# Two-layer graph network: nine upper products move into the first pass over the adjacency, and GpSimd folds part of the row sums

## The chip, the cores and the metric

The kernel runs on one core of a Trainium2 chip. The metric is the device time of one execution in microseconds. Three runs before the change gave a median of 897.39 (895.74 to 899.43).

## The reference

```python
A = adj + I                                # adj: 4096 x 4096, f32
d = rsqrt(sum(A, axis=1))
x1 = layernorm(x + elu(((A * d[:, None] * d[None, :]) @ x) @ w))
x2 = layernorm(x1 + relu((adj @ x1) @ W.T + b))     # x: 4096 x 256
```

## The kernel before

The 4096 nodes are cut into 8 groups of 512 (32-row blocks are dealt out so that two groups share one panel of 1024). A **chunk** is the part of adj with one row group and one panel of 1024 columns, 2.1 MB, in one of the tiles raw0 to raw2; SyncE and ScalarE each issue two of its four transfers (`load_chunk`, L248). A chunk holds two **units** (row group, column group), 512 by 512 each. There are 64 units in each of the two layers.

A unit goes through three engines. VectorE turns it in 32 by 32 blocks (`turn`, L530, one STREAM_TRANSPOSE). ScalarE copies it to the rounded a_hi (`hi`, L378), and VectorE writes the rest, a_lo (`lo`, L549), two halves each. TensorE makes 24 products of 128x512 into one accumulator (`product`, L802): v_hi with a_hi, v_hi with a_lo, v_lo with a_hi. v is the right factor, in a high and a low part: y = d * (x @ w) in the first layer, x1 in the second. Each of turned, a_hi and a_lo has two buffers, so VectorE runs at most two units ahead of TensorE.

The chunks come in three passes, each a list built at L63 to L94.
- Pass A, chunks 0 to 31, reads all of adj once for the degrees. VectorE sums DVE_BLOCKS blocks of a chunk (`deg_part`, L560) and ScalarE the rest of the 16 (L388). At the end of a row group VectorE adds the parts (`deg_sum`), TensorE folds them over the partitions (`fold_degrees`, L733), VectorE adds 1 (`deg_row`), GpSimd makes d (L336), ScalarE scales x @ w by it and rounds it to v_hi (`make_y`, L398), and VectorE makes v_lo (`v_low`, L582). As row group r gives v of group r, pass A can take the units below the diagonal: those with a column group before the row group, 28 in all, and one diagonal unit, (0, 0). Their accumulators are kept in the tile partial (`keep_partial`, L417). x @ w of a group is made on TensorE in `turn_x` and `project_x`.
- Pass B, chunks 32 to 63, reads all of adj again: the other 35 units of layer 1 complete a row group of x1 each, and behind them come the 28 units of layer 2 below the diagonal.
- Pass C, 20 chunks, does the 36 units of layer 2 on and above the diagonal.

When a row group is complete, VectorE aggregates (L588), TensorE projects it (L764), ScalarE makes the elu, the moments and the normalised rows, GpSimd adds x (L346) and makes the small factors, each at a fixed number of units behind (AGG_AT and the others, L132).

Every engine runs its own list in a written order; semaphores hold an engine until its input is there. SyncE and ScalarE issue the loads of a chunk when the chunk before it in the same buffer has been turned and summed (`raw_free`, L253). SyncE's queue also carries the loads of x, each behind a fixed chunk (L297).

## Time and profile before

| | |
|---|---|
| median of 3 runs | 897.39 us (895.74 to 899.43) |
| the profiled execution | 896.96 us |
| its span, first to last instruction | 894.9 us |
| TensorE (PE) busy | 790.3 us, 88% |
| VectorE (DVE) | 738.4 us, 83% |
| ScalarE (ACT) | 528.5 us, 59% |
| GpSimd (POOL) | 102.5 us, 11% |
| HBM read | 185.2 MB, 212 GB/s over the span |

Busy time is the time in which an engine executes. A matmul is pipelined, so a busy TensorE need not be at its peak. A row of a timeline gives start and duration in us, engine, line (L556 is line 556), the tiles written and read, and in brackets the idle time before it with what ended it. "x2" is two instructions shown together.

### The profile page before, as it was taken

The page shows a single profiled execution, that of the slowest core. Times are in us where ns is not written, and L with a number is a line of the kernel's source. Part 1 is how long each engine was busy: PE and PEld are TensorE (multiplying, and loading weights), DVE is VectorE, ACT ScalarE, POOL GpSimd, SP SyncE. Part 2 cuts the span into 40 slices and gives each one's busy share as a digit, 9 for nine tenths or more (in the row PEclk, how much of TensorE's full clock was granted, in tenths as well). Part 3 has the DMA queues.
Part 4 walks back from the last instruction along what each step waited for, and adds up shares of the span by engine and source line. Part 5 has one row for each costly group of instructions (what it writes and reads, how often), then busy time and mean ns, then how long its engine had stood idle before and what let it go on. Part 6 is the DMA issues. An engine that isn't in the chain of part 4 may idle for free. (4 is left out here: it accounts for less than half of the span.)

```text
span 894.9 us, 10620 instructions
## 1 busy us (share of the span) xinstructions
PE 790.3 (88%) x3532; PEld 650.9 (73%) x3532; DVE 738.4 (83%) x557; ACT 528.5 (59%) x1180; POOL 102.5 (11%) x109
## 2 busy tenths in 40 slices
PE   0166477698999999999999999999999999999996
PEld 0045365577888788888888888888887878888884
DVE  0749478889998889898989889898979889888863
ACT  1447377578877544756667575756744665455361
POOL 0000000000000000211112021110210412022020
PEclk9987698899999999999999999999999999999998
DMA  9999999988975997878888787888895897997800
GB/s 273 305 294 287 304 210 301 276 208 251 247 214 162 237 210 217 194 180 191 225 190 214 191 223 182 192 224 192 200 242 170 193 229 187 222 214 178 222 24 23
DMA packets 192037, 190.09 MB, mean 212 GB/s; under 512 B 7024, under 2 KB 191984, under 8 KB 191984
## 3 DMA queue, kind: packets, MB, share of 16 engines
q1 hardware_dynamic: 98928, 97.40, 42.8%
q10 hardware_dynamic: 93056, 92.03, 41.6%
q8 instruction: 28, 0.46, 0.2%
q14 instruction: 25, 0.20, 0.1%
HBM read 185.20 MB, written 4.19 MB: 212 GB/s over the span
## 5 line engine op out<-in xcount | busy, mean ns | idle before, releaser
L820 PE MATMUL acc<-a_hi,v_hi 128*128 128x512 f32 x1024 | 408.3, 399 | 17.5 <-DVE a_lo L556 13.3
L385 ACT ACTIVATE a_hi<-turned 128x1024 fp32r<-128x1024 f32 x256 | 264.5, 1057 | 260.9 <-PE acc L822 130.1
L821 PE MATMUL acc<-a_lo,v_hi 128*128 128x512 f32 x1024 | 402.9, 393 | 0.0
L822 PE MATMUL acc<-a_hi,v_lo 128*128 128x512 f32 x1024 | 402.7, 393 | 0.0
L539 DVE STREAM_TRANSPOSE turned<-raw 128x2048 f32<-128x2048 f32 x128 | 294.1, 2305 | 46.1 <-DMA raw<-in_adj_dram 39.0
L556 DVE TENSOR_TENSOR a_lo<-turned,a_hi 128x1024 fp32r<-128x1024 f32 x256 | 301.9, 1217 | 33.2 <-ACT a_hi L385 16.7
L820 PEld LDWEIGHTS acc<-a_hi,v_hi 128*128 128x128 f32 x1024 | 195.1, 191 | 61.9 <-issue 17.3
L822 PEld LDWEIGHTS acc<-a_hi,v_lo 128*128 128x128 f32 x1024 | 194.8, 190 | 41.3
L821 PEld LDWEIGHTS acc<-a_lo,v_hi 128*128 128x128 f32 x1024 | 195.2, 191 | 39.8
L395 ACT ACTIVATE acc<-raw 128x256 f32<-128x256 f32 x236 | 87.0, 368 | 27.7 <-issue 22.3
L563 DVE TENSOR_REDUCE deg_parts<-raw 128x10 f32<-128x2560 f32 (+4 forms) x32 | 77.9, 2442 | 9.5 <-DMA raw<-in_adj_dram 9.5
L346 POOL TENSOR_TENSOR raw<-raw,x_row 128x1024 f32<-128x1024 f32 x8 | 22.1, 2761 | 223.3 <-ACT raw L441 223.3
L739 PE MATMUL acc<-deg_sums,fold 128*32 128x4 f32 x64 | 2.1, 194 | 48.5 <-DVE deg_sums L572 48.5
L395 ACT ACTIVATION_READ_ACCUMULATOR acc<-raw 128x1 f32 x236 | 44.3, 188 | 0.0
L336 POOL TENSOR_TENSOR dinv<-deg,minus_half 128x4 f32<-128x4 f32 x8 | 11.0, 1375 | 283.4 <-DVE deg L580 283.4
L585 DVE TENSOR_TENSOR v_lo<-normed,v_hi 128x1024 fp32r<-128x1024 f32 x16 | 19.6, 1224 | 25.1 <-ACT v_hi L474 17.5
L739 PEld LDWEIGHTS acc<-deg_sums,fold 128*32 128x32 f32 x64 | 1.4, 124 | 51.0 <-DVE deg_sums L572 50.6
L458 ACT ACTIVATE raw<-raw,minus_mean 128x256 f32<-128x256 f32 x60 | 29.8, 499 | 12.2 <-issue 6.4
L470 ACT ACTIVATE normed<-raw,shift,rstd 128x256 f32<-128x256 f32 x60 | 31.2, 591 | 6.3 <-POOL shift L368 6.3
L359 POOL TENSOR_SCALAR minus_mean<-sums 128x4 f32<-128x4 f32 x15 | 9.6, 643 | 219.4 <-ACT raw L452 219.4
L760 PE MATMUL proj<-w_sb,x_row 128*128 128x256 f32 x128 | 30.5, 393 | 1.1 <-ACT x_row L414 1.1
L760 PEld LDWEIGHTS proj<-w_sb,x_row 128*128 128x128 f32 x128 | 25.1, 198 | 5.1 <-ACT x_row L414 1.4
(56 smaller groups left out, 353.0 us busy)
## 6 DMA issues: line engine op xcount, KB each, us to landing
raw<-in_adj_dram SPq DMA_DIRECT2D x168, 512.0 KB, 8.8
raw<-in_adj_dram ACTq DMA_DIRECT2D x168, 512.0 KB, 9.8
x_row<-in_x_dram SPq DMA_DIRECT2D x64, 128.0 KB, 6.7
out_dram<-normed ACTq DMA_DIRECT2D x28, 128.0 KB, 3.1
w_sb<-in_L_gnn_w_dram SPq DMA_DIRECT2D x1, 256.0 KB, 15.7
normed<-in_L_gnn_W_dram SPq DMA_DIRECT2D x1, 256.0 KB, 14.1
out_dram<-normed SPq DMA_DIRECT2D x4, 64.0 KB, 1.8
out_dram<-normed ACTq DMA_DIRECT2D x4, 64.0 KB, 1.9
```

Of the source, the lines that this page charges most:

```text
L346: nc.gpsimd.tensor_tensor(res, res, x_row[:], ALU.add).then_inc(s_resx, 1)
L385: nc.scalar.activation(a_hi[u % 2][:, part, :], turned[u % 2][:, part, :], ACT.Copy).then_inc(s_hi, 1)
L395: nc.scalar.activation(junk[:, i % JUNK, :], raw[buffer_of[n]][:, k, :], ACT.Copy, accum_out=deg_parts[:, row % 2, panel, k:k + 1]).then_i ...
L458: nc.scalar.activation(neg[:, t, :], res[:, t, :], ACT.Square, bias=minus_mean[:, t:t + 1], accum_out=squares[:, t:t + 1]).then_inc(s_sq, 1)
L470: nc.scalar.activation(normed[:, t, :], res[:, t, :], ACT.Identity, scale=rstd[:, t:t + 1], bias=shift[:, t:t + 1]).then_inc(s_norm, 1)
L539: ins = nc.vector.transpose(dst, src)
L556: nc.vector.tensor_tensor(a_lo[u % 2][:, part, :], turned[u % 2][:, part, :], a_hi[u % 2][:, part, :].bitcast(F32), ALU.subtract).then_inc ...
L563: nc.vector.tensor_reduce(deg_parts[:, row % 2, panel, mine], raw[buffer_of[n]][:, mine, :], AX_X, ALU.add).then_inc(s_degd, 1)
L760: ins = pe.matmul(proj[:, t, :], flat[:, GN * h + P * t:GN * h + P * (t + 1)], w_sb[:, h, :], start=(h == 0), stop=(h == CH - 1))
L820: pe.matmul(dst, v_hi[:, k, ch], a_hi[u % 2][:, t, :], start=begin, stop=False)
L821: pe.matmul(dst, v_hi[:, k, ch], a_lo[u % 2][:, t, :], start=False, stop=False)
L822: ins = pe.matmul(dst, v_lo[:, k, ch], a_hi[u % 2][:, t, :], start=False, stop=end)
```

## The change

Pass A takes ten of the units on and above the diagonal, those whose row and column group are both below 4 (one of them, (0, 0), was there before); so it has 38 units and pass B 54 of two layers in 28 chunks. FIRST_UNITS is the table of what is done at which chunk. A unit above the diagonal is done at a later chunk than its own, when v of its column group exists. Its chunk is kept until then: chunks (0, 1), (1, 1), (0, 0) and (2, 1) lie in three further places, in the upper parts of v_hi, v_lo and partial that pass A does not use before, and others stay in a rotating buffer for up to two chunks more. Six accumulators are added onto a partial that is there already (`add_partial`, VectorE).

In groups 0 to 3, `make_y` and the low half of v (`y_low`) come at the end of the own row group, since the last unit needs them. v_hi is written from PSUM in one step, and v_lo by four operations that scale x @ w again. From group 2 on GpSimd adds halves of four of the 16 blocks of each chunk in three steps (256 columns to 32, `fold_part`), and VectorE reduces what is left (`deg_of_pool`). VectorE has 10, 10, 8, 6, 5, 6, 6, 5 blocks per row group in place of 10, 10, 10, 9, 9, 8, 7, 6, and ScalarE 6, 6, 4, 6, 7, 6, 6, 7 in place of 6, 6, 6, 7, 7, 8, 9, 10. ScalarE issues its share of a load by a list, `loads_at`.

```diff
+    FAST = 4
     chunks = []
     units = []
     accs = []
-    def add_chunk(name, row, panel, columns):
-        chunks.append((name, row, panel, []))
+    visits = []
+    def add_unit(name, row, col, n, visit):
+        layer = 0 if name == "A" or (name == "B" and col >= row) else 1
+        if not accs or accs[-1][:3] != (name, row, layer):
+            accs.append((name, row, layer, len(units), None))
+        accs[-1] = accs[-1][:4] + (len(units),)
+        visits[visit].append(len(units))
+        units.append((name, row, col, n, len(accs) - 1))
+    def add_chunk(name, row, panel, columns=()):
+        chunks.append((name, row, panel))
+        visits.append([])
         for col in columns:
-            layer = 0 if name == "A" or (name == "B" and col >= row) else 1
-            if not accs or accs[-1][:3] != (name, row, layer):
-                accs.append((name, row, layer, len(units), None))
-            accs[-1] = accs[-1][:4] + (len(units),)
-            chunks[-1][3].append(len(units))
-            units.append((name, row, col, len(chunks) - 1, len(accs) - 1))
-    DIAGONALS = 1
-    ORDER_A = [[1, 2, 3, 0], [1, 2, 3, 0], [2, 0, 3, 1], [2, 0, 3, 1], [2, 0, 3, 1], [0, 3, 1, 2], [0, 3, 1, 2],
+            add_unit(name, row, col, len(chunks) - 1, len(chunks) - 1)
+    ORDER_A = [[1, 2, 3, 0], [1, 2, 3, 0], [0, 2, 3, 1], [0, 2, 3, 1], [2, 0, 3, 1], [0, 3, 1, 2], [0, 3, 1, 2],
                [0, 1, 2, 3]]
+    FIRST_UNITS = {3: [(0, 0)], 7: [(1, 0)], 8: [(1, 1)], 9: [(0, 1), (2, 0)], 10: [(2, 1)], 12: [(2, 2)],
+                   13: [(0, 2), (1, 2)], 14: [(3, 0), (3, 1)], 15: [(3, 2)], 16: [(3, 3), (0, 3)],
+                   17: [(1, 3), (2, 3)], 18: [(4, 0), (4, 1)], 19: [(4, 2), (4, 3)]}
     for row in range(GROUPS):
         for panel in ORDER_A[row]:
-            add_chunk("A", row, panel, [col for col in (2 * panel, 2 * panel + 1)
-                                        if col < row or col == row < DIAGONALS])
-    for row in range(GROUPS):
-        own = row // 2
-        for panel in ([*range(own + 1, PANELS), own, *range(own)] if row else range(PANELS)):
-            both = [col for col in (2 * panel, 2 * panel + 1) if not col == row < DIAGONALS]
-            add_chunk("B", row, panel, both[::-1] if panel == own and row % 2 else both)
+            add_chunk("A", row, panel)
+    chunk_of = {(row, panel): n for n, (_, row, panel) in enumerate(chunks)}
+    for n, (_, row, panel) in enumerate(list(chunks)):
+        here = FIRST_UNITS.get(n, []) if row <= FAST else [(row, c) for c in (2 * panel, 2 * panel + 1) if c < row]
+        for r, col in here:
+            add_unit("A", r, col, chunk_of[r, col // 2], n)
+    LATE = range(FAST // 2, PANELS)
+    for row, panels in ((0, LATE), (1, LATE), (2, LATE), (1, (0,)), (3, LATE), (2, (0,)), (4, (3, 2)), (3, (0, 1)),
+                        (4, (0, 1)), (5, (3, 2, 0, 1)), (6, (3, 0, 1, 2)), (7, (3, 0, 1, 2))):
+        for panel in panels:
+            both = [c for c in (2 * panel, 2 * panel + 1) if row >= FAST or panel in LATE or c < row]
+            add_chunk("B", row, panel, both[::-1] if panel == row // 2 and row % 2 else both)
...
+    adds = [a for a, s in enumerate(accs) if s[0] == "A" and any(k[:2] == s[:2] for k in accs[:a])]
+    partials = [a for a in range(len(accs)) if a not in rows_done and a not in adds]
...
+    HOMES = {chunk_of[0, 1]: 3, chunk_of[1, 1]: 4, chunk_of[0, 0]: 5, chunk_of[2, 1]: 5}
     buffer_of, before, filled = [], [], []
-    for n, c in enumerate(chunks):
-        buffer_of.append(n % 3 if n <= THIRD + 2 else (n - THIRD - 1) % 2)
-        held = [k for k in range(n) if buffer_of[k] == buffer_of[n]]
+    for n in range(len(chunks)):
+        if n in HOMES:
+            home = HOMES[n]
+        else:
+            held = [max([k for k in range(n) if buffer_of[k] == i], default=-1) for i in range(3)]
+            free = [(done_at[k] if k >= 0 else -1, i) for i, k in enumerate(held)]
+            home = min(free[:3 if n <= FIRST_B else 2])[1]
...
+    AHEAD = 3
+    loads_at = [[] for _ in chunks]
+    for n in range(AHEAD, len(chunks)):
+        loads_at[max(n - AHEAD, -1 if before[n] is None else done_at[before[n]])].append(n)
+    DVE_BLOCKS = [10, 10, 8, 6, 5, 6, 6, 5]
+    POOL_BLOCKS, POOL_FROM = 4, 2 * PANELS
+    ACT_BLOCKS = [RB - d - (POOL_BLOCKS if row >= 2 else 0) for row, d in enumerate(DVE_BLOCKS)]
...
+        late = FAST * GT * C
+        raw.append(nc.alloc_sbuf_tensor_at("held0", [P, RB, STRIPE], F32, offset=v_at + 4 * late))
+        raw.append(nc.alloc_sbuf_tensor_at("held1", [P, RB, STRIPE], F32, offset=v_at + 4 * (N // P * C + late)))
+        raw.append(partial[:, FAST:, :, :].rearrange("p g h n -> p (g h n)").rearrange("p (b m) -> p b m", b=RB))
...
+                if n >= POOL_FROM:
+                    eng.wait_ge(s_halved, n - POOL_FROM + 1)
...
+                    n = PANELS * m + (1 if m < FAST else 2)
...
+            def fold_part(n):
+                i = n - POOL_FROM
+                raw_loaded(pool, n)
+                mine = raw[buffer_of[n]][:, RB - POOL_BLOCKS:, :]
+                if i:
+                    pool.wait_ge(s_quartered, i)
+                nc.gpsimd.tensor_tensor(halved[:], mine[:, :, :STRIPE // 2], mine[:, :, STRIPE // 2:], ALU.add).then_inc(s_halved, 1)
+                pool.wait_ge(s_halved, i + 1)
+                if i:
+                    pool.wait_ge(s_folded, i)
+                nc.gpsimd.tensor_tensor(quartered[:], halved[:, :, :STRIPE // 4], halved[:, :, STRIPE // 4:], ALU.add).then_inc(s_quartered, 1)
+                pool.wait_ge(s_quartered, i + 1)
+                if i >= 2:
+                    pool.wait_ge(s_degp, i - 1)
+                nc.gpsimd.tensor_tensor(folded[:, i % 2, :, :], quartered[:, :, :STRIPE // 8], quartered[:, :, STRIPE // 8:],
+                                        ALU.add).then_inc(s_folded, 1)
...
+            for n in range(FIRST_B):
+                row, at = divmod(n, PANELS)
+                if n >= POOL_FROM:
+                    fold_part(n)
+                if row < FAST and at == PANELS - 1:
+                    make_dinv(row)
+                if row > FAST and at == 0:
+                    make_dinv(row - 1)
...
                 act.wait_ge(s_xw, row + 1)
-                if row:
-                    act.wait_ge(s_v, row)
+                if row >= FAST:
+                    act.wait_ge(s_turn, max(units_through[n] for n in HOMES))
                 for t in range(GT):
-                    ins = nc.scalar.activation(normed[:, t, :], proj[:, t, :], ACT.Copy,
+                    ins = nc.scalar.activation(v_hi[:, tiles(row).start + 2 * t, :], proj[:, t, :], ACT.Copy,
                                                scale=dinv[:, GT * row + t:GT * row + t + 1])
-                ins.then_inc(s_yf, 1)
-                act.wait_ge(s_yf, row + 1)
-                nc.scalar.activation(v_hi[:, tiles(row), :], normed[:], ACT.Copy).then_inc(s_vhi, 1)
+                ins.then_inc(s_vhi, 1)
...
+            for n in range(AHEAD):
+                load_chunk(act, n, (2, 3))
+            for n in range(FIRST_B):
+                row, at = divmod(n, PANELS)
+                summed_first = row < FAST and at == PANELS - 1
+                if summed_first:
+                    raw_loaded(act, n)
+                    deg_part(n)
+                if n == PANELS - 1:
+                    make_y(row)
+                for u in visits[n]:
+                    hi_and_later(u)
+                    if u == visits[n][0] and row > FAST and at == Y_AT:
+                        make_y(row - 1)
+                if not visits[n] and row > FAST and at == Y_AT:
+                    make_y(row - 1)
+                if not summed_first:
+                    raw_loaded(act, n)
+                    deg_part(n)
+                load_others(n)
+                if summed_first and n > PANELS:
+                    make_y(row)
+                if at == (2 if row < FAST else 3):
+                    keep_xt(row)
+            for n in range(FIRST_B, len(chunks)):
+                for u in visits[n]:
+                    if u == visits[n][-1]:
+                        load_others(n)
...
+            def y_low(row):
+                dve.wait_ge(s_vhi, row + 1)
+                for t in range(GT):
+                    k = tiles(row).start + 2 * t
+                    ins = nc.vector.scalar_tensor_tensor(out=v_lo[:, k, :], in0=proj[:, t, :],
+                                                         scalar=dinv[:, GT * row + t:GT * row + t + 1],
+                                                         in1=v_hi[:, k, :].bitcast(F32), op0=ALU.mult, op1=ALU.subtract)
+                ins.then_inc(s_v, 1)
+            def add_partial(a):
+                row = accs[a][1]
+                dve.wait_ge(s_used, halves_of(accs[a][4], 1))
+                dve.wait_ge(s_part, partial_of[next(k for k in partials if accs[k][:2] == accs[a][:2])] + 1)
+                if add_of[a]:
+                    dve.wait_ge(s_padd, add_of[a])
+                nc.vector.tensor_tensor(partial[:, row, :, :], acc[bank_of[a]][:], partial[:, row, :, :],
+                                        ALU.add).then_inc(s_padd, 1)
 
             def v_low(i, row):
...
+            def turn_and_low(u):
+                turn(u)
+                if u:
+                    low_and_later(u - 1)
             dve.wait_ge(s_const, 1)
 
-            for n, (name, row, panel, mine) in enumerate(chunks):
-                done, at = divmod(n, PANELS)
-                last = done - 1
-                if 0 <= last < GROUPS and at == (1 if last < DIAGONALS else 3):
-                    v_low(last, last)
+            for n in range(FIRST_B):
+                row, at = divmod(n, PANELS)
+                if n > POOL_FROM and at:
+                    deg_of_pool(n - 1)
+                if 0 < row <= FAST and at == 0:
+                    y_low(row - 1)
+                if row > FAST and at == 3:
+                    y_low(row - 1)
+                if row < FAST and at == PANELS - 1:
+                    raw_loaded(dve, n)
+                    deg_part(n)
+                    deg_sum(row)
+                    if row < 2:
+                        deg_row(row)
+                    for u in visits[n]:
+                        turn_and_low(u)
+                        low_and_later(u)
+                    if row >= 2:
+                        deg_row(row)
+                else:
+                    for u in visits[n]:
+                        if units[u][3] == n:
+                            raw_loaded(dve, n)
+                        turn_and_low(u)
+                    raw_loaded(dve, n)
+                    deg_part(n)
+                    if n == 1:
+                        keep_wt()
+                    if row > FAST and at == 0:
+                        deg_row(row - 1)
+                    if visits[n]:
...
+            for n in range(FIRST_B):
+                row, at = divmod(n, PANELS)
+                if row < FAST and at == 2:
+                    turn_x(row)
+                if row < FAST and at == 3:
+                    project_x(row)
+                    fold_degrees(row)
+                for u in visits[n]:
+                    if row >= FAST and u == last_in_a[row]:
                         fold_degrees(row)
                     product(u)
-                    for a in ended(u, PROJECT_AT, rows_done):
-                        project(a)
-                if name == "A" and n % PANELS == (1 if row < DIAGONALS else 2):
+                if row >= FAST and at == 2:
```

In the order of instructions on VectorE, row group 3 of pass A (chunks 12 to 15) reads as follows before. L580 is deg of group 2, L585 the low half of v for group 2.

```order
L563 TENSOR_REDUCE deg_parts<-raw 128x9
L580 TENSOR_SCALAR deg<-acc 128x4
L539 STREAM_TRANSPOSE turned<-raw 128x2048 x2
L556 TENSOR_TENSOR a_lo<-turned,a_hi 128x1024 x2
L563 TENSOR_REDUCE deg_parts<-raw 128x9
L556 TENSOR_TENSOR a_lo<-turned,a_hi 128x1024 x2
L563 TENSOR_REDUCE deg_parts<-raw 128x9
L585 TENSOR_TENSOR v_lo<-normed,v_hi 128x4x256
L539 STREAM_TRANSPOSE turned<-raw 128x2048
L563 TENSOR_REDUCE deg_parts<-raw 128x9
```

The end of group 2 and the first two chunks of the same group 3 after the change. L672 is deg of group 2, L679 its low half, L652 the reduction of what GpSimd folded, held_49 and held_50 the chunks kept in v_hi and v_lo.

```order
L664 TENSOR_REDUCE deg_sums<-deg_parts 128x16
L672 TENSOR_SCALAR deg<-acc 128x4
L679 SCALAR_TENSOR_TENSOR v_lo<-proj,dinv,v_hi 128x256 x4
L621 STREAM_TRANSPOSE turned<-partial 128x2048
L628 TENSOR_TENSOR turned<-turned,ident 128x4x32 x4
L645 TENSOR_REDUCE deg_parts<-raw 128x6
L638 TENSOR_TENSOR a_lo<-turned,a_hi 128x1024 x2
L652 TENSOR_REDUCE deg_parts<-folded 128x4
L621 STREAM_TRANSPOSE turned<-held_49 128x2048
L621 STREAM_TRANSPOSE turned<-held_50 128x2048
L638 TENSOR_TENSOR a_lo<-turned,a_hi 128x1024 x2
```

The low half has moved from behind three chunks' reductions to the place right behind deg, ahead of the first transpose of group 3.

On ScalarE, the same place before: x_row is kept, the first chunk of group 3 summed, two units of a_hi, a partial, a sum, a load, and then `make_y` (L405, L409) of group 2.

```order
L414 ACTIVATE x_row<-proj 128x1024
L395 ACTIVATE acc,deg_parts<-raw 128x256 x7
L251 DMA raw<-in_adj_dram 32x16x256 x2
L385 ACTIVATE a_hi<-turned 128x1024 x4
L423 ACTIVATE partial<-acc 128x1024
L395 ACTIVATE acc,deg_parts<-raw 128x256 x7
L251 DMA raw<-in_adj_dram 32x16x256 x2
L405 ACTIVATE normed<-proj,dinv 128x256 x4
L409 ACTIVATE v_hi<-normed 128x4x256
```

And after: chunk 11 is summed from partial, and `make_y` (L472) of group 2 follows it.

```order
L479 ACTIVATE x_row<-proj 128x1024
L462 ACTIVATE acc,deg_parts<-partial 128x256 x4
L287 DMA raw<-in_adj_dram 32x16x256 x2
L472 ACTIVATE v_hi<-proj,dinv 128x256 x4
L452 ACTIVATE a_hi<-turned 128x1024 x2
```

`make_y` stands ahead of all of group 3's units, and its second step is gone.

## Rows read from the trace of the kernel before

**Rows 1.** The page, TensorE's busy tenths in 40 equal slices of the span.
```profile
PE   0166477698999999999999999999999999999996
```

**Rows 2.** Busy us by engine (x instructions), TensorE's clock, DMA share, GB/s, three stretches.
```profile
50.00:175.00 125.00, 77.71 (x333) 62.46 (x332) 88.34 (x54) 76.36 (x243) 3.80 (x6) 0.82 1.07 281
175.00:300.00 125.00, 120.16 (x567) 98.57 (x567) 113.44 (x81) 95.65 (x276) 7.81 (x8) 1.00 0.81 220
300.00:850.00 550.00, 547.29 (x2448) 453.67 (x2447) 494.55 (x373) 322.74 (x563) 79.14 (x71) 1.00 0.85 204
```

**Rows 3.** Timeline of VectorE: start us, us, operation, [idle before <- releaser].
```profile
66.69 2.31 DVE L539 STREAM_TRANSPOSE turned<-raw 128x2048 f32<-128x2048 f32 x1 [6.76 <-DMA raw<-in_adj_dram]
88.22 2.35 DVE L556 TENSOR_TENSOR a_lo<-turned,a_hi 128x1024 fp32r<-128x1024 f32 x2
176.88 4.50 DVE L539 STREAM_TRANSPOSE turned<-raw 128x2048 f32<-128x2048 f32 x2
296.11 2.30 DVE L539 STREAM_TRANSPOSE turned<-raw 128x2048 f32<-128x2048 f32 x1
```

**Rows 4.** Timeline of GpSimd and TensorE; third row from the groups by form.
```profile
397.68 2.96 POOL L346 TENSOR_TENSOR raw<-raw,x_row 128x1024 f32<-128x1024 f32 x1 [23.22 <-ACT raw L441]
593.13 2.97 POOL L346 TENSOR_TENSOR raw<-raw,x_row 128x1024 f32<-128x1024 f32 x1 [23.44 <-ACT raw L441]
L779 PE MATMUL proj<-ident,raw 128*128 128x128 f32 x64 | 8.3, 272 | 0.0
184.08 3.61 PE L760 MATMUL proj<-w_sb,x_row 128*128 128x256 f32 x16
302.02 3.61 PE L760 MATMUL proj<-w_sb,x_row 128*128 128x256 f32 x16
```

**Rows 5.** VectorE's groups by form: line, operation, shapes xcount | busy us, mean ns | idle.
```profile
L539 DVE STREAM_TRANSPOSE turned<-raw 128x2048 f32<-128x2048 f32 x128 | 294.1, 2305 | 46.1 <-DMA raw<-in_adj_dram 39.0 <-DVE a_lo L556 0.5
L556 DVE TENSOR_TENSOR a_lo<-turned,a_hi 128x1024 fp32r<-128x1024 f32 x256 | 301.9, 1217 | 33.2 <-ACT a_hi L385 16.7 <-issue 11.4 <-PE acc L822 3.5
L563 DVE TENSOR_REDUCE deg_parts<-raw 128x10 f32<-128x2560 f32 x12 | 33.5, 2809 | 6.5 <-DMA raw<-in_adj_dram 6.5
L563 DVE TENSOR_REDUCE deg_parts<-raw 128x6 f32<-128x1536 f32 x4 | 7.0, 1738 | 0.0
L605 DVE TENSOR_TENSOR raw<-acc,partial 128x512 f32<-128x512 f32 x30 | 19.2, 682 | 0.0
L546 DVE TENSOR_TENSOR turned<-turned,ident 128x128 f32<-128x128 f32 x32 | 7.2, 287 | 0.3
L572 DVE TENSOR_REDUCE deg_sums<-deg_parts 128x16 f32<-128x64 f32 x8 | 2.1, 257 | 3.6 <-issue 3.6
L681 DVE SCALAR_TENSOR_TENSOR raw<-acc,x_row 128x256 f32<-128x256 f32 x4 | 1.7, 419 | 0.7 <-PE acc L848 0.7
```

**Rows 6.** Timeline of the first group's degrees, 47 to 52 us.
```profile
47.96 1.02 POOL L336 TENSOR_TENSOR dinv<-deg,minus_half 128x4 f32<-128x4 f32 x1 [45.03 <-DVE deg L580]
49.07 0.24 POOL L338 TENSOR_SCALAR ndinv<-dinv 128x4 f32<-128x4 f32 x1
50.56 1.57 ACT L405 ACTIVATE normed<-proj,dinv 128x256 f32<-128x256 f32 x4 [2.60 <-PE proj L760]
```

**Rows 7.** The page, DMA issues: KB each, median us from issue to landing.
```profile
raw<-in_adj_dram ACTq DMA_DIRECT2D x168, 512.0 KB, 9.8
```

**Rows 8.** Timeline of GpSimd and VectorE where a GpSimd add meets VectorE.
```profile
437.30 2.31 DVE L539 STREAM_TRANSPOSE turned<-raw 128x2048 f32<-128x2048 f32 x1
439.54 1.57 DVE L556 TENSOR_TENSOR a_lo<-turned,a_hi 128x1024 fp32r<-128x1024 f32 x1
695.14 2.40 POOL L352 TENSOR_TENSOR x_row<-v_hi,v_lo 128x1024 f32<-128x1024 f32 x1
696.05 3.72 DVE L556 TENSOR_TENSOR a_lo<-turned,a_hi 128x1024 fp32r<-128x1024 f32 x2
```

**Rows 9.** Busy us by engine over one row group of the second pass.
```profile
385.00:424.00 39.00, 39.00 (x177) 32.36 (x177) 36.29 (x30) 25.89 (x45) 5.53 (x5) 1.00 0.80 192
```

More of the change, by code:

```diff
@@ L105, in gnn_two_layers @@
     partial_of = {a: i for i, a in enumerate(partials)}
-    THIRD = next(n for n, c in enumerate(chunks) if c[0] == "B" and n % 3 == 2)
-    buffer_of, before, filled = [], [], []
-    for n, c in enumerate(chunks):
-        buffer_of.append(n % 3 if n <= THIRD + 2 else (n - THIRD - 1) % 2)
-        held = [k for k in range(n) if buffer_of[k] == buffer_of[n]]
+    add_of = {a: i for i, a in enumerate(adds)}
+    units_through = [max([u + 1 for u in range(U) if units[u][3] == n], default=0) for n in range(len(chunks))]
@@ L248, in load_chunk @@
         def load_chunk(eng, n, qs):
-            _, row, panel, _ = chunks[n]
+            _, row, panel = chunks[n]
             for q in qs:
@@ L633, in low_and_later @@
                 lo(u)
+                for a in ended(u, AGG_AT, adds):
+                    add_partial(a)
                 for a in ended(u, AGG_AT, rows_done):
```

146 lines of the change are left out of this document (74 added, 72 removed).

## The prediction

> **What bounds the kernel now.** I read the slices first, then the busy time of three stretches, then single instructions. In [rows 1] TensorE is nearly idle at the left, rises to six or seven tenths and is full from about the eighth slice on. [rows 2] puts numbers to it. From 175 us on TensorE works 667.5 of 675 us: everything behind that point lasts as long as TensorE has work. From 50 to 175 us it works 77.7 of 125 us. There VectorE works 88.3 us and the DMA engines move 281 GB/s, nearly their most; its waits for a chunk are of the kind of the first row of [rows 3]. So there are two phases with different limits: one where chunks and degrees arrive too slowly for TensorE, and one where TensorE is the limit with VectorE just behind it (494.6 of 550 us). The change moves nine products (units) from the second phase to the first. The sum is therefore: what the second phase loses, less what the first gets longer.
>
> **What the second phase loses.** In [rows 4] the residual add of GpSimd comes at 397.68 and, five row groups later, at 593.13, which is 39.1 us per group. In these five groups TensorE does seven units per group and one set of eight transposes into proj. Those take about 1.0 (eight at 0.27 that overlap, as the eight of x take 1.03 in the trace at full clock). (39.1 - 1.0) / 7 = 5.43 us per unit. Nine units fewer behind chunk 31: 9 x 5.43 = **48.9 us**. TensorE's total work does not change, as 128 units stay 128. That four of 84 chunks need not be loaded again gives nothing of its own: behind 300 us the DMA engines are at 0.85 [rows 2] and TensorE is not waiting for them. Had they been the limit, four chunks of 2.1 MB at 204 GB/s would be 41 us, less than the 49 that TensorE gives, so the loads do not become the limit either.
>
> **What the first phase gets longer.** I follow VectorE chunk by chunk, since it takes part in every step. Costs, from [rows 3, 5]: a transpose 2.25 (two take 4.50); the two subtractions 2.27 (2.35 less the overlap), so a unit 4.52; a reduction of 10 blocks 2.81 and of 6 blocks 1.74, hence 0.27 per block and 2.2 for the 8 of group 2, 1.7 for the 6 of group 3, 1.4 for the 5 of group 4; four diagonal adds 0.85; an add of an accumulator onto its partial, an operation that the trace of before does not show in this shape, like the two halves of L605, 1.25 (bounds 1.0 and 1.4); the new low half from PSUM like four of L681, 1.4 with overlap (bounds 1.2 and 1.7; the old one was one instruction of 1.2); the reduction of what GpSimd folded, next to deg_sums at 0.26, 0.2 to 0.3.
> The start: six chunks have buffers of their own now and VectorE's first reduction no longer stands behind the copy of the weights, but the chunks still come at the DMA rate. Chunk 7, at 66.69 before, I put at 64. From there reduction, sum, fold on TensorE, dinv on GpSimd (1.02 + 0.24) and v_hi on ScalarE (1.57) [rows 6] bring VectorE to chunk 8 at about 73.5.
> Chunks 8 to 19 without a gap: 18 units at 4.52 are 81.4; reductions 4 x (2.2 + 1.7 + 1.4) = 21.2; twelve small ones 2.4; six adds 7.5; three low halves 4.2; three diagonals 2.6; sums and degrees 0.8. Together 120 us, so chunk 20 would be begun at 193.6.
> The gaps: in groups 0 to 3 the row group's own v is now needed by its last unit, so its low half stands ahead of all else on VectorE in the next chunk. At the end of group 2 VectorE is through with chunk 11 at 104.8. TensorE still has the unit of chunk 10 (its low half at 100.7, so until 105.3), then the projection of x (3.61, [rows 4]) and the fold: 109.5. Then VectorE 0.2, GpSimd 1.35, ScalarE 1.57: the low half starts at 112.8, and VectorE has stood for 8 us. Behind it are queued all transposes of group 3, and TensorE waits for those. At the end of group 3 the fold comes in time, and 3.3 us of the same chain are bare, with 1 us for a_hi of chunk 15. Nearly 13 us in all. TensorE waits twice more for an adder (unit 9 for that of unit 7, unit 16 for that of unit 14), 2 us each, which later work does not feel as VectorE is the later one. So VectorE begins chunk 20 at **207**, and not at 176.88 [rows 3]. TensorE's last projection of that stage ends 9 us behind it, at 216, where it ended at 187.7 before (184.08 + 3.61): 28.5 later.
> Are chunks there in time? A buffer is held for a later column up to three chunks long, so that of the three rotating ones two remain at times. A load takes 9.8 us from issue to landing on ScalarE's queue, in the median [rows 7]. The tightest are chunk 11 (ScalarE issues its half at 92, so it lands at about 102 and is wanted at 102) and chunk 18 (issued at 170, lands at 180, wanted at 183). I take no wait, with up to 3 us each at a few of them as the upper bound.
> Groups 5 to 7: 18 units as before. From 187.7 to 305.6 (302.02 + 3.61) TensorE took 117.9, of which 4.9 idle [rows 2]. The same work, a smaller reduction on VectorE (17 blocks x 4 x 0.27 instead of 21 x 4, 4.3 less, and 3 more for the folds) and v_hi in one step on ScalarE: 116. The second pass starts 26.6 us later.
> GpSimd's folds: a fold is three adds of 512, 256 and 128. The add of 1024 alone takes 2.41 [rows 8], so 1.2 + 0.6 + 0.3 = 2.1 us. While that of 695.14 runs, VectorE's two subtractions take 3.72 and not 2.35, and at 439.54 one takes 1.57 and not 1.22; the transpose of 437.30 under the same add stays at 2.31. So an operation with two inputs from SBUF waits for GpSimd's to end, one with a single input does not. Such operations are some 40% of VectorE's time here: 0.3 us per fold, 3 us for the twelve on VectorE's path. The Trainium skill (GPSIMD Engine Reference, Key points) says that GpSimd shares its SBUF interfaces with VectorE and contends with instructions that have two SBUF inputs. By that rule, too, transposes go free, and the trace agrees (3.72 against 2.31).
> The second pass: rows 0, 1 and 2 of layer 1 now end four units apart and not seven. ScalarE is busy 25.9 of 39 us in a group [rows 9]; without three units (2.1 each) and a kept partial (1.0), 18.5 of the 22.7 us that four units take, and with loads to issue and waits between the norm's steps it is full. VectorE: 4 x 4.52 and 5.5 for aggregate, residual, low half and its wait for v_hi, 23.6 of 22.7. One us in each of three groups: 3 us.
>
> **Sum.** 894.9 + 26.6 - 48.9 + 3 + 3 = 878.6 of span; the profiled execution took 2.1 us more than its span and lies 0.4 below the median of the runs, so 881; the steps are good to a few us, and the walk leans on full delays, so I say **880**.
>
> **Rivals.**
> A, the phase takes the units in nearly free. For it: TensorE idles 47 us of those 125, and VectorE 37. Against it: three small chains at the group ends, which nothing covers. Without the 13 us of gaps the end is 880 - 13 = 867. Chance 0.28.
> B, GpSimd's folds hold VectorE. If each of 24 folds fell wholly into two-input work it would cost VectorE 2.1 us, 50 in all, in place of the 3 in the sum, and the end would be 877 + 50 = 927, slower than before. It decides from (897 - 877) / 24 = 0.8 us per fold on. Against it: most of a fold falls on transposes and reductions, with one input. Chance 0.08.
> C, chunks arrive late. Two free buffers, so a load begins only when its predecessor is read; if half of the twelve chunks come 3 us late, 18 us more: 898, no change. For it is the 281 GB/s of before, against it that a chunk is now wanted every 10 us and not every 8. Chance 0.10.
> D, the crowded epilogues. If ScalarE falls behind by 4 us in each of the three groups and TensorE stands still as long: 889. Chance 0.12. That the units do not move is no rival: the order of instructions shows 38 products ahead of the first of the second pass, and 29 before.
>
> **Chances.** The forecast 0.42 (870 to 890). What this measurement can tell from no change is 0.5%, 4.5 us. Faster: the forecast and A whole, most of D, a part of C: 0.80. Same: the middle of C and the edges, 0.11. Slower: B and the far end of C, 0.09. Range 861 to 898.
>
> **What would show it.** VectorE should begin the first transpose of chunk 20 between 200 and 212; the second pass's first transpose, at 296.11 before [rows 3], comes some 27 us later, near 323. TensorE's granted clock from 50 to 175 should be above 0.82, as it stands idle less. A gap of VectorE of 7 to 9 us ahead of the third low half of v shows the chain; none there speaks for A. Subtractions above 1.5 us beside L378 show B; waits of VectorE for DMA in groups 2 to 4 show C; idle time of TensorE in the first 60 us of the second pass shows D. Wrong would be the whole reading if the part behind chunk 31 did not shrink by nine units' time.

## The result and the profile after

Over eight fast runs of each, the changed kernel takes 889.34 us (886.75 to 894.12) and the kernel before 895.43 (893.84 to 899.43). The ratio is 0.9926, with a 95% interval of 0.9904 to 0.9947, so it is 6 to 7 us faster. The forecast was 880, 16 to 17 us faster. The profiled executions have spans of 885.5 and 894.9 us. Medians in different comparisons differ by up to 3 us for the kernel before, so experiments are compared by their ratio to it. A single trace places an event less well than its two decimals suggest: up to the end of group 7's projection, the run y7_early below executes the same program as the changed kernel, and its trace has group 4's projection end 1.2 us later and group 7's 3.5 us later.

First the page and the same three stretches as [rows 1, 2]; columns as there.

```profile
PE   0446959799999999899999999999999989999996
```

```profile
50.00:175.00 125.00, 92.84 (x390) 74.81 (x391) 101.06 (x96) 62.80 (x174) 34.18 (x36) 0.84 0.85 211
175.00:300.00 125.00, 122.26 (x571) 100.78 (x570) 122.58 (x103) 80.86 (x212) 42.70 (x44) 1.00 0.90 239
300.00:850.00 550.00, 541.12 (x2418) 447.26 (x2417) 487.40 (x369) 326.44 (x603) 84.08 (x78) 0.99 0.82 200
```

TensorE works 15 us more in the first stretch, and the DMA engines move 211 GB/s there, down from 281. The chunks no longer set the stage: from chunk 8 to chunk 19 VectorE waits for none. In the third stretch, however, TensorE has become idle for 8.9 us, where it was idle for 2.7. The slices show half of it as the 8 at the 17th place, 354 to 376 us, where [rows 1] has a 9.

The ends of TensorE's projections of x divide the time. For group 4, group 7 and the end of the span they are at 187.7, 305.6 and 894.9 before, and at 224.1, 337.7 and 885.5 after:

```profile
220.44 3.61 PE L905 MATMUL proj<-w_sb,x_row 128*128 128x256 f32 x16
334.73 2.97 PE L905 MATMUL proj<-w_sb,x_row 128*128 128x256 f32 x13
```

So groups 0 to 4 take 36.4 us more (forecast 28.5, and 3 for the folds), groups 5 to 7 take 113.6 and not 117.9 (forecast 116), and what follows takes 547.8 instead of 589.3: 41.5 less, where nine units should have taken away 48.9. The sum is 36.4 - 4.3 - 41.5 = -9.4 us of span.

Where the first stage went, on VectorE (the third low half of v, the last sums of group 4 with the first transpose of chunk 20, the first transpose of the second pass; compare [rows 3]) and TensorE:

```profile
114.44 0.16 DVE L672 TENSOR_SCALAR deg<-acc 128x4 f32<-128x4 f32 x1 [4.46 <-PE acc L884]
117.67 1.66 DVE L679 SCALAR_TENSOR_TENSOR v_lo<-proj,dinv,v_hi 128x256 fp32r<-128x256 f32 x4 [3.07 <-ACT v_hi L472]
214.37 0.26 DVE L664 TENSOR_REDUCE deg_sums<-deg_parts 128x16 f32<-128x64 f32 x1
214.55 2.30 DVE L621 STREAM_TRANSPOSE turned<-raw 128x2048 f32<-128x2048 f32 x1
328.19 2.30 DVE L621 STREAM_TRANSPOSE turned<-raw 128x2048 f32<-128x2048 f32 x1
```

```profile
65.79 5.50 PE L905 MATMUL proj<-w_sb,x_row 128*128 128x256 f32 x16 [5.65 <-ACT x_row L479]
125.42 0.77 PE L967 MATMUL acc<-a_hi,v_hi 128*128 128x512 f32 x1 [11.05 <-DVE a_lo L638]
125.98 0.63 PE L968 MATMUL acc<-a_lo,v_hi 128*128 128x512 f32 x1
126.41 0.63 PE L969 MATMUL acc<-a_hi,v_lo 128*128 128x512 f32 x1
```

VectorE's gap at the end of group 2 is there as forecast, 4.46 + 3.07 = 7.5 us. TensorE stands still for 11.05 us at the same place, for the chain of the degrees, the low half, a transpose, four diagonal adds, a reduction and a subtraction. Its matmuls then start 0.43 us apart, at a granted clock of 0.50 (1.2 GHz), where those at full clock are 0.23 apart.

The second pass, where the forecast had no such gap (unit 41, the first with column group 7):

```profile
356.90 1.65 DVE L679 SCALAR_TENSOR_TENSOR v_lo<-proj,dinv,v_hi 128x256 fp32r<-128x256 f32 x4
358.47 2.30 DVE L621 STREAM_TRANSPOSE turned<-raw 128x2048 f32<-128x2048 f32 x1
```

```profile
358.61 0.80 PE L967 MATMUL acc<-a_hi,v_hi 128*128 128x512 f32 x1 [4.57 <-DVE v_lo L679]
359.20 0.63 PE L968 MATMUL acc<-a_lo,v_hi 128*128 128x512 f32 x1
366.00 0.39 PE L969 MATMUL acc<-a_hi,v_lo 128*128 128x512 f32 x1
```

v_lo of group 7 is made at chunk 35, behind the a_lo of unit 42. Unit 41 waits for it. The second pass of before began with column groups 1 to 3 and needed group 7 two chunks later; the change sends it straight to column groups 4 to 7 and left the low half of group 7 at FIRST_B + 3. Unit 41 itself lasts from 358.61 to 366.23, 7.6 us and not 5.4, since its first matmuls run at the lower clock. The same stall, 4.6 to 5.0 us long, is in the traces of all eight kernels here that have this order and this place of the low half, and in none of the three that make it earlier.

Part of its length may come from a load. VectorE had waited for chunk 33 before it came to the low half:

```profile
338.42 2.31 DVE L621 STREAM_TRANSPOSE turned<-raw 128x2048 f32<-128x2048 f32 x1 [3.42 <-DMA raw<-in_adj_dram]
```

Without this wait it would not have been there a full 3.4 us sooner, as the a_lo of unit 42 needs the buffer of unit 40, and TensorE begins the last matmul of unit 40 at 353.65. An estimate from these rows is that the late chunk made the stall longer by at most 1.8 us. No run changes this load by itself.

### The profile page after: what moved, and what is told of

Its sections match the earlier page's. It is cut to its first block and busy times, and to the rows that moved or that the text cites. A ratio compares the mean times of both kernels' runs of the same rounds, so it can differ in the third digit from the quotient of the medians.

```text
span 885.5 us, 10755 instructions
## 1 busy us (share of the span) xinstructions
PE 793.9 (90%) x3532; PEld 652.4 (74%) x3532; DVE 745.8 (84%) x611; ACT 501.5 (57%) x1084; POOL 172.7 (20%) x181
## 5 line engine op out<-in xcount | busy, mean ns | idle before, releaser
L638 DVE TENSOR_TENSOR a_lo<-turned,a_hi 128x1024 fp32r<-128x1024 f32 x256 | 307.9, 1240 | 32.3 <-ACT a_hi L452 24.2
L621 DVE STREAM_TRANSPOSE turned<-raw 128x2048 f32<-128x2048 f32 x120 | 275.4, 2302 | 26.8 <-DMA raw<-in_adj_dram 21.3
L462 ACT ACTIVATE acc<-raw 128x256 f32<-128x256 f32 x170 | 62.7, 369 | 24.5 <-DMA raw<-in_adj_dram 21.4
L645 DVE TENSOR_REDUCE deg_parts<-raw 128x6 f32<-128x1536 f32 (+3 forms) x28 | 53.5, 1911 | 18.1 <-DMA raw<-in_adj_dram 18.1
L378 POOL TENSOR_TENSOR halved<-raw 128x512 f32<-128x512 f32 x23 | 31.0, 1348 | 107.2 <-DMA raw<-in_adj_dram 107.2
L905 PE MATMUL proj<-w_sb,x_row 128*128 128x256 f32 x128 | 33.8, 424 | 13.2 <-ACT x_row L479 13.2
L905 PEld LDWEIGHTS proj<-w_sb,x_row 128*128 128x128 f32 x128 | 27.4, 216 | 18.7 <-ACT x_row L479 13.9
L462 ACT ACTIVATION_READ_ACCUMULATOR acc<-raw 128x1 f32 x170 | 31.9, 188 | 0.0
L519 ACT ACTIVATE raw<-raw 128x256 f32<-128x256 f32 x60 | 24.1, 403 | 5.2 <-DVE raw L738 2.7
L926 PE MATMUL proj<-wt_sb,raw 128*128 128x256 f32 x112 | 25.3, 379 | 0.0
```

What stands on the lines that cost most here:

```text
L378: nc.gpsimd.tensor_tensor(halved[:], mine[:, :, :STRIPE // 2], mine[:, :, STRIPE // 2:], ALU.add).then_inc(s_halved, 1)
L462: nc.scalar.activation(junk[:, i % JUNK, :], raw[buffer_of[n]][:, k, :], ACT.Copy, accum_out=deg_parts[:, row % 2, panel, k:k + 1]).then_i ...
L621: ins = nc.vector.transpose(dst, src)
L638: nc.vector.tensor_tensor(a_lo[u % 2][:, part, :], turned[u % 2][:, part, :], a_hi[u % 2][:, part, :].bitcast(F32), ALU.subtract).then_inc ...
L645: nc.vector.tensor_reduce(deg_parts[:, row % 2, panel, mine], raw[buffer_of[n]][:, mine, :], AX_X, ALU.add).then_inc(s_degd, 1)
L905: ins = pe.matmul(proj[:, t, :], flat[:, GN * h + P * t:GN * h + P * (t + 1)], w_sb[:, h, :], start=(h == 0), stop=(h == CH - 1))
```

## Experiments

**v of group 7 earlier (y7_early).**

```diff
-                    if u == visits[n][0] and n == FIRST_B + Y_AT:
+                    if u == visits[n][0] and n == FIRST_B + 1:
...
-                if n == FIRST_B + 3:
+                if n == FIRST_B + 2:
                     y_low(GROUPS - 1)
```

> The changed kernel with v of group 7 one chunk earlier in the second pass (v_hi on ScalarE at chunk 33, v_lo on VectorE at chunk 34). Theory 1 (the second pass loses time because unit 41, the first that needs column group 7, comes two chunks earlier than before while v_lo of group 7 stayed at its old chunk): TensorE's gap of 4.57 us at unit 41 and the 2.2 us that this unit takes longer at the lower clock go, so about 882.5 us, 7 below the changed kernel's 889.3, ratio to before about 0.985. Theory 2 (the rest of the second pass is paced by the closer epilogues, so that what is won here is lost within the next ten units): 887 to 890.

Measured: 883.94 us, ratio 0.9838 (0.9818 to 0.9858), 0.9% below the changed kernel, 8 us by the ratios (5 to 10 by their intervals). The low half now stands ahead of the transpose of unit 42, on VectorE:

```profile
351.23 1.65 DVE L679 SCALAR_TENSOR_TENSOR v_lo<-proj,dinv,v_hi 128x256 fp32r<-128x256 f32 x4
352.79 2.30 DVE L621 STREAM_TRANSPOSE turned<-raw 128x2048 f32<-128x2048 f32 x1
```

TensorE works the whole stretch from 350 to 375, first fence; the second is the changed kernel's:

```profile
350.00:375.00 25.00, 25.00 (x117) 20.77 (x116) 24.63 (x22) 10.72 (x11) 0.00 (x0) 1.00 0.76 204
```

```profile
350.00:375.00 25.00, 20.43 (x81) 16.43 (x80) 19.24 (x19) 8.19 (x11) 0.00 (x0) 0.86 0.55 154
```

Theory 1 holds. The run also measures the closer epilogues: from the end of group 7's projection (341.2) to the end of the span (881.9) are 540.7 us, 7.1 less than in the changed kernel and 48.6 less than the 589.3 of before. The three traces with this edit have 540.4 to 542.0 us there, the eight of the changed kernel and its variants without it 546.0 to 550.0. The closer epilogues cost nothing that can be seen.

**Without the folds (no_folds).** GpSimd's folds are left out, and VectorE reads 32 columns of the raw blocks; the other 224 columns of these blocks are left out of the degrees. A buffer comes free when VectorE has read it.

```diff
                 if n >= POOL_FROM:
-                    eng.wait_ge(s_halved, n - POOL_FROM + 1)
+                    eng.wait_ge(s_degp, n - POOL_FROM + 1)
...
-                if n >= POOL_FROM:
-                    fold_part(n)
...
-                dve.wait_ge(s_folded, i + 1)
-                nc.vector.tensor_reduce(..., folded[:, i % 2, :, :],
+                raw_loaded(dve, n)
+                nc.vector.tensor_reduce(..., raw[buffer_of[n]][:, RB - POOL_BLOCKS:, 0:STRIPE // 8],
```

> The changed kernel without GpSimd's folds: VectorE sums only the first 32 columns of the four blocks that GpSimd folded, so the degrees lack the rest; the reduction on VectorE has the same size. Theory 1 (folds cost VectorE the few subtractions that wait for GpSimd: some 1.1 us at four or five places in groups 2 to 4): the first pass gets 3 to 5 us shorter, about 885.5. Theory 2 (folds hold every chunk, 0.8 us each on 24 chunks): 870. Theory 3 (they fall where VectorE has slack): 889, as the changed kernel.

Measured: 886.3 us, ratio 0.9872 (0.9859 to 0.9886), 0.54% below 0.9926, or 4.8 us, and the intervals are apart. In size that is theory 1, 3 to 5 us. The traces do not show it in the first pass, where theory 1 has it: the spans differ by only 1.5 us, group 4's projection ends 0.4 us earlier than in the changed kernel and group 7's 0.3 later. So the folds cost between nothing and 5 us, and theory 2 is out. In the changed kernel a fold is 1.35 + 0.89 + 0.72 = 3.0 us on average, with the time in which VectorE holds it. One of the two largest holds of VectorE, in the middle of group 4:

```profile
197.32 1.31 POOL L378 TENSOR_TENSOR halved<-raw 128x512 f32<-128x512 f32 x1 [5.99 <-DMA raw<-in_adj_dram]
197.97 3.42 DVE L638 TENSOR_TENSOR a_lo<-turned,a_hi 128x1024 fp32r<-128x1024 f32 x2
198.71 1.60 POOL L382 TENSOR_TENSOR quartered<-halved 128x256 f32<-128x256 f32 x1
200.39 1.32 POOL L386 TENSOR_TENSOR folded<-quartered 128x128 f32<-128x128 f32 x1
```

The two subtractions take 3.42 and not 2.35, as in [rows 8].

**The folds alone (folds_alone).** The kernel before with `fold_part`, `deg_of_pool` and the new split.

```diff
-    DVE_BLOCKS = [10, 10, 10, 9, 9, 8, 7, 6]
+    DVE_BLOCKS = [10, 10, 8, 6, 5, 6, 6, 5]
+    POOL_BLOCKS, POOL_FROM = 4, 2 * PANELS
```

> The kernel before with GpSimd's folds and the new split of the blocks, and the units, buffers and places of v as before. Theory 1 (the folds and the split alone give a little, since VectorE sums 13 blocks fewer per panel, 13 x 4 x 0.27 = 14 us less work, but most of that in the first stage where it waits for chunks): 890 to 895. Theory 2 (the loads set that stage, so the split is worth nothing, and the folds cost): 895 to 900.

Measured: 892.29 us, ratio 0.9939 (0.9919 to 0.9959), 5 to 6 us faster than before, within theory 1. Group 4's projection ends at 189.7, 2.0 later than before; groups 5 to 7 take 113.6 us (to 303.3, the row below), as in the changed kernel, and not 117.9. Most of the gain lies in these groups, which the forecast had at 2 us.

```profile
299.68 3.61 PE L808 MATMUL proj<-w_sb,x_row 128*128 128x256 f32 x16
```

**The units alone (units_alone).** The changed kernel with the old split and no folds.

```diff
-    DVE_BLOCKS = [10, 10, 8, 6, 5, 6, 6, 5]
+    DVE_BLOCKS = [10, 10, 10, 9, 9, 8, 7, 6]
...
-    ACT_BLOCKS = [RB - d - (POOL_BLOCKS if row >= 2 else 0) for row, d in enumerate(DVE_BLOCKS)]
+    ACT_BLOCKS = [RB - d for row, d in enumerate(DVE_BLOCKS)]
```

> The changed kernel without GpSimd's folds and with the split of the blocks of before (VectorE 10, 10, 10, 9, 9, 8, 7, 6, ScalarE the rest): the units, the kept chunks and the places of v alone. Theory 1 (TensorE and the degree chains at the group ends set the first stage, as light_sums left chunk 20 at 214.5 us): the 10 us more of sums on VectorE in groups 2 to 4 cost at most 3 us, less the 3 that the folds cost, so 889 to 894 and a ratio near 0.993, as with the folds. Theory 2 (VectorE's work sets it after all, and light_sums was held by a fold or a load): 9 blocks x 4 x 0.27 = 10 us later, 900.

Measured: 897.83 us, ratio 1.0008 (0.9987 to 1.003). The nine units, as they were moved, are worth nothing without the folds and the new split; theory 1 was off by 7 us in the time, which came nearer to theory 2's 900, and right in the stage it spoke of. Group 4's projection ends at 227.0, only 3 us behind the changed kernel's 224.1. Most of the rest was lost in groups 5 to 7, 119.6 us up to 346.6. In the traces with the new split and TensorE's and VectorE's full work these groups take 113.6 to 115.9 us, in the two with the old split 117.9 and 119.6. no_folds, which has the new split without the folds, has 114.4, so the gain here looks like the split's.

```profile
343.03 3.61 PE L896 MATMUL proj<-w_sb,x_row 128*128 128x256 f32 x16
```

**Less work for VectorE (light_sums), for TensorE (third_product_out), for both (both_lightened).** The first leaves blocks out of the sums in groups 2 to 4, the second the products with v_lo in units 2 to 19, the third both.

```diff
+    DVE_DONE = [10, 10, 1, 1, 1, 6, 6, 5]
...
-                mine = slice(0, DVE_BLOCKS[row])
+                mine = slice(0, DVE_DONE[row])
```

```diff
+                        light = 2 <= u <= 19
-                        ins = pe.matmul(dst, v_lo[:, k, ch], a_hi[u % 2][:, t, :], start=False, stop=end)
+                        if not light:
+                            ins = pe.matmul(dst, v_lo[:, k, ch], a_hi[u % 2][:, t, :], start=False, stop=end)
```

> The changed kernel where VectorE sums one block instead of 8, 6 and 5 in groups 2 to 4 (the other blocks are left out of the degrees): 4 x (7 + 5 + 4) x 0.27 = 17 us less work on VectorE between chunk 8 and chunk 19. Theory 1 (VectorE's row of work sets these twelve chunks, 130 us for 120 us of work): chunk 20 is begun 13 to 17 us earlier than 214.6, and the end is near 889.3 - 13 = 876, a little less than the work, as TensorE then becomes the later one. Theory 2 (arrival of the chunks or the chain of the degrees sets them): 885 to 889.

> The changed kernel where units 2 to 19 leave out their eight products with v_lo: 18 x 8 x 0.227 = 32.7 us less work for TensorE up to chunk 19, nothing else changed (the output lacks these products). Theory 1 (TensorE's queue sets the first stage wherever it is not waiting for a degree chain): VectorE then becomes the later one with its 120 us of work and the two chain gaps; chunk 20 is begun at 203 to 208 and not at 214.6, and the stage ends up to 14 us earlier, so 875 to 880. Theory 2 (VectorE's walk is the limit as forecast): 886 to 889.

> The changed kernel with both cuts at once: VectorE sums one block in groups 2 to 4, and units 2 to 19 have no products with v_lo (both left out of the output). Each alone brought chunk 20 forward by at most 2 us. Theory 1 (VectorE and TensorE are two queues of the same length here, so that one alone frees nothing): together they bring the end of group 4's projection from 224 to 212 or less, and the time to 872 to 878, more than the 5 to 7 us that the two gave one by one. Theory 2 (neither is the limit, the arrival of chunks or ScalarE is): 884 or more, the sum of the two at best.

Measured: 888.03 us (0.9891, 0.9876 to 0.9906), 886.27 (0.9881, 0.986 to 0.9902) and 879.18 (0.9809, 0.9776 to 0.9842). From 0.9926 that is 3, 4 and 10.5 us. The first is not clear of the noise, and that both together give more than the sum of the two is not shown by the times (10.5 against 7, at an interval of 3 us to either side). The traces show it. The last deg_sums of group 4, light_sums, third_product_out and both_lightened in this order; the changed kernel's is at 214.37:

```profile
214.29 0.27 DVE L665 TENSOR_REDUCE deg_sums<-deg_parts 128x16 f32<-128x64 f32 x1 [0.39 <-ACT acc L463]
```

```profile
212.29 0.26 DVE L664 TENSOR_REDUCE deg_sums<-deg_parts 128x16 f32<-128x64 f32 x1
```

```profile
204.15 0.26 DVE L665 TENSOR_REDUCE deg_sums<-deg_parts 128x16 f32<-128x64 f32 x1
```

17 us of work less on VectorE does not move chunk 20 at all, 33 us less on TensorE (at full clock) moves it by 2, and both move it by 10. The end of group 4's projection moves by +1.8, -2.3 and -12.0 us. Theory 1 of both_lightened holds in the trace (212.0, forecast 212 or less) and misses its time by 1 us (879.18, forecast 872 to 878); theory 1 of each of the others alone falls. third_product_out alone would have read as its theory 2, VectorE's walk as the limit; light_sums excludes that. There are two queues of nearly the same length. Of TensorE's 33 us only 22 went off its busy time between 77 and 214 us (116.1 to 94.3): the granted clock of this stretch fell from 0.90 to 0.86, and the matmuls that were left took longer.

Two limits of this reading. From the low half of group 2 to that of group 3 even both cuts win nothing (46.4 us in the changed kernel, 46.2 in both_lightened); all is won in groups 2 and 4. At the end of group 3 VectorE waits for ScalarE's sums, which neither edit touches:

```profile
151.15 0.27 DVE L665 TENSOR_REDUCE deg_sums<-deg_parts 128x16 f32<-128x64 f32 x1 [2.66 <-ACT acc L463]
```

And of the 12 us by which both_lightened is ahead at group 4's projection, 6 are lost again in groups 5 to 7, which take 119.6 us there; what holds them is not shown.

Busy times of the changed kernel and of light_sums from 118 to 214 us:

```profile
118.00:214.00 96.00, 81.17 (x352) 66.01 (x352) 89.57 (x80) 54.56 (x140) 26.77 (x28) 0.90 0.71 179
```

```profile
118.00:214.00 96.00, 80.00 (x342) 65.18 (x343) 80.59 (x79) 53.92 (x139) 23.45 (x24) 0.90 0.68 170
```

VectorE's 9 us of saved work became 9 us of waiting, 5 of them at the end of group 3 for a chunk, a fold and ScalarE's sums; TensorE's busy time is nearly the same.

**A unit into the gap (unit_behind_fold).**

```diff
-    FIRST_UNITS = {..., 9: [(0, 1), (2, 0)], 10: [(2, 1)], ...}
+    FIRST_UNITS = {..., 9: [(0, 1), (2, 0)], 11: [(2, 1)], ...}
...
-                    if row < 2:
+                    if row < 3:
                         deg_row(row)
...
-                    if row >= 2:
+                    if row >= 3:
                         deg_row(row)
```

> The changed kernel where unit (2, 1) comes at chunk 11 instead of chunk 10, behind the fold of group 2, and the degree of group 2 is taken ahead of it. TensorE then projects x and folds the degrees 5.4 us earlier or as soon as the sums are there (109.7 us), and has this unit to do in the gap of 11 us. Theory 1 (the gap at unit 6 is lost time): its 11 us shrink to 4 to 6, so 883 to 885, ratio 0.986. Theory 2 (chunk 8 held one chunk longer delays chunk 14's load, and that costs as much): 888 to 892.

Measured: 889.56 us, ratio 0.9918 (0.9899 to 0.9936): no change. The gap is split in two, and the sixth unit starts at the same time:

```profile
115.02 0.77 PE L967 MATMUL acc<-a_hi,v_hi 128*128 128x512 f32 x1 [5.01 <-DVE a_lo L638]
125.06 0.77 PE L967 MATMUL acc<-a_hi,v_hi 128*128 128x512 f32 x1 [2.96 <-DVE a_lo L638]
```

```profile
117.32 1.64 DVE L679 SCALAR_TENSOR_TENSOR v_lo<-proj,dinv,v_hi 128x256 fp32r<-128x256 f32 x4
```

The expectation counted TensorE's gap as the loss, but that unit was TensorE's only other work. The degree of group 2 was there 4.4 us earlier (110.08), but ScalarE and VectorE then did the moved unit's a_hi and a_lo ahead of v, so that the low half starts at 117.32 and not at 117.67: group 2's v is there at the same time. The time lies in theory 2's range, but its cause, a late load of chunk 14, is not seen: after chunk 11, VectorE waits for no chunk of the first pass.

**A transpose into VectorE's wait (turn_first).**

```diff
-                        turn_and_low(u)
+                        turn(u)
+                        if early and u == visits[n][0]:
+                            y_low(row - 1)
+                        low_and_later(u - 1)
```

> The changed kernel where the first unit of groups 2 to 4 is turned before the low half of v (chunks 8, 12 and 16), so that VectorE does this transpose in the 3.07 us in which it waits for ScalarE's v_hi. Theory 1 (TensorE's gaps of 11.05 us at unit 6 and 6.1 us at unit 12 are lost time, as is the lower clock behind them): about 3 us shorter at each of them, so 884, 5 below the changed kernel, ratio 0.986 to 0.989. Theory 2 (the backlog of TensorE behind the gap takes it back, since VectorE is ahead by two units at once): 888 to 890.

Measured: 887.66 us, ratio 0.9902 (0.9882 to 0.9921), 2 us less; the intervals overlap, so the times alone do not show a gain, and theory 1 gave 5. The traces agree with the sign: the gaps are 8.83 and 4.23 us instead of 11.05 and 6.13, and group 4's projection ends at 221.3, 2.8 earlier.

**Edits together (chain_short and chain_short_no_fold_edit).** y7_early and turn_first, and in the first also the fold ahead of the projection:

```diff
                 if row < FAST and at == 3:
+                    if row >= 2:
+                        fold_degrees(row)
                     project_x(row)
-                    fold_degrees(row)
+                    if row < 2:
+                        fold_degrees(row)
```

> The changed kernel with three edits of order: v of group 7 one chunk earlier (as y7_early), the first unit of a group turned before the low half of v (as turn_first), and in groups 2 and 3 the fold of the degrees ahead of the projection of x on TensorE. Theory 1 (the degree chains at the ends of groups 2 and 3 cost TensorE 17 us of gaps, and the edits take 3 and 2 us off each; the stall at unit 41 is apart from that): y7_early's 882 less 2 for turn_first and 2 to 3 for the fold, 877 to 879, ratio 0.979. Theory 2 (behind the gaps the two full queues take the rest back): 881 to 883, as y7_early.

> As chain_short, but the projection stays ahead of the fold in groups 2 and 3. If the fold ahead of the projection is worth something, this is 2 to 3 us slower than chain_short, 880; if v_hi waits for the projection anyway, it is the same.

Measured: 876.63 us, ratio 0.9784 (0.9758 to 0.981), and 879.28, ratio 0.9809 (0.9783 to 0.9835). The first is the fastest kernel of this study, 19 us below before and 1.4% below the changed one by the ratios. It was to be near 0.979 and is. The fold edit alone can't be told from nothing: the intervals overlap widely, and the spans are 875.7 and 875.1. Its trace has shorter gaps (below, against 8.87 and 3.63 without it) but group 4's projection ends at 220.0 and 219.8.

```profile
123.66 0.76 PE L971 MATMUL acc<-a_hi,v_hi 128*128 128x512 f32 x1 [6.70 <-DVE a_lo L638]
168.00 0.47 PE L971 MATMUL acc<-a_hi,v_hi 128*128 128x512 f32 x1 [2.88 <-DVE a_lo L638]
```

## Why the prediction was wrong

The sign and the order of the terms were right, the size was not: 6 to 7 us in place of 16 to 17. In spans, 885.5 in place of 878.6, so 6.9 us are to be explained. Two steps failed by about as much: the second pass (4.4 us) and what the first phase gets longer (5 us); groups 5 to 7 gave 2.4 us back.

1. "What the second phase loses", 48.9 us, was right as TensorE's time: y7_early shows 48.6, and the two other traces with its edit 47.3 and 48.9.
2. "The second pass" is the step whose mechanism failed. It priced the crowded epilogues at 3 us, which turned out as nothing, and did not follow the change's new order of column groups to their v. Unit 41 needs group 7 two chunks earlier than its counterpart did. Together 41.5 us were won and not 45.9, so 4.4 us of the miss. The stall costs 6.8 us in the trace (4.57 waiting, 2.2 at the lower clock) and 8 by the ratios of y7_early. With it mended the kernel is at 0.9838 of before, and the forecast of 880 against 897.39 was 0.981.
3. "What the first phase gets longer" was mis-sized, by as much: chunk 20 was begun at 214.55, forecast 207, and the projection ended at 224.1, forecast 216. Half of that came early. Chunk 7 was begun at 65.58 and not at 64, the fold of group 1 stood behind a projection of 5.50 us (3.61 at full clock), for which VectorE waited 2.83, and so the second low half came at 77.6. That was to be 73.5. The rest came from held subtractions (2.2 us in group 4) and a wait of 2.1 for ScalarE's sums. Since the folds' 3 us stood in the sum apart, this is 5 us of the miss. The second pass's first transpose, forecast near 323, is at 328.19.
4. The reading behind this walk, that VectorE is the later one and TensorE's waits are not felt, is refuted by light_sums. That the walk still came within 8 us is in part luck: TensorE's queue, which it did not follow, is about as long.
5. Groups 5 to 7 were forecast at 116 us and took 113.6. In this trace 2.4 us came back; y7_early has 115.9 for the same work, so this can be chance. That the new split is worth some us there is shown by more traces than one: 117.9 and 119.6 without it, 113.6 to 115.9 with it.
6. The folds' price on VectorE, 3 us, lies between what no_folds shows, 1.5 in the spans and 4.8 by the ratios. A fold is 3.0 us long, not 2.1, and 2.5 where nothing holds it. Rival B, from 0.8 us for each of 24 folds on, did not come.
7. Of the other rivals, A did not come: the gap of VectorE that was to show the chain is there with 7.5 us, and groups 0 to 4 took longer, not less, than forecast. C did not come: VectorE waited for no chunk from chunk 8 to chunk 19. D's idle time of TensorE was there, in the first 25 us of the second pass, but by another mechanism than D's. What the last paragraph named as a sign against the whole reading, a second pass that does not shrink by nine units, was the sign that counted.

folds_alone and units_alone, 0.6% and 0.0%, make up the 0.74% of the change between them. chain_short finds another 0.5% behind y7_early, in the first stage.

What stays open: whether the folds cost 5 us or nothing, what holds group 3 when both queues are lightened, and which order of units would be the best for both queues.

## What to carry to other kernels

When units of work are moved between passes, follow every input of the first units that remain, not only of those moved: here a factor made at a fixed chunk was needed two chunks earlier, and this took about half of the gain (8 us, where 6 to 7 were left). Where two engines are filled to the same level, taking work off one shows nothing; only a cut on both, or on the chain between them, tells. And a gap is lost time only if the work put into it was late elsewhere.

## What was not expected of the hardware

A chain of adds on GpSimd does not halve with its size. Where nothing holds them, the adds of 512, 256 and 128 elements take 1.31, 0.74 and 0.47 us in the changed kernel, so the last step of the fold costs a third of the first for a quarter of the elements:

```profile
149.67 1.31 POOL L378 TENSOR_TENSOR halved<-raw 128x512 f32<-128x512 f32 x1 [15.54 <-DMA raw<-in_adj_dram]
151.06 0.74 POOL L382 TENSOR_TENSOR quartered<-halved 128x256 f32<-128x256 f32 x1
151.88 0.47 POOL L386 TENSOR_TENSOR folded<-quartered 128x128 f32<-128x128 f32 x1
```

Beside subtractions of VectorE the same two last steps take up to 1.83 and 1.36 us.

The gaps of TensorE of 4.57 and 11.05 us were paid twice here. The matmuls behind them are at half the clock, 0.43 us apart in place of 0.23, for 4.4 us behind the first and 5.6 behind the second; unit 41 took 2.2 us longer by it.
